# First cross attention: division by the row sums moved from VectorE and TensorE to GpSimd, and the small jobs dealt to other units

## The reference

```python
Q = (x @ WQ_w.T + WQ_b).reshape(b, sq, H, DK).transpose(0, 2, 1, 3)
K = (kv @ WK_w.T + WK_b).reshape(b, sk, H, DK).transpose(0, 2, 1, 3)
V = (kv @ WV_w.T + WV_b).reshape(b, sk, H, DK).transpose(0, 2, 1, 3)
T = jnp.einsum('bhqd,bhkd->bhqk', Q, K) / math.sqrt(DK)
T = T + attn_bias[:, None, :, :]
T = jnp.where(m2[:, None, :, :] == 0, -1000000000.0, T)
A = jax.nn.softmax(T, axis=-1)
out = jnp.einsum('bhqk,bhkd->bhqd', A, V)
out = out.transpose(0, 2, 1, 3).reshape(b, sq, E)
return out @ WO_w.T + WO_b
```

## Time and profile before

| | us |
|---|---|
| median of 3 runs | 2248.33 (2246.73 to 2257.74) |
| the profiled execution | 2246.41 |
| its span | 2244.6 |
| of it the first attention | 0 to 346.6 |
| first scores of batch 1, of batch 2, of batch 3 | 101.48, 179.53, 257.58 |

### The profile page before, as it was taken

One profiled execution on the slowest core, in us unless ns is written; L12 is line 12 of the kernel. 1 busy time (PEld: TensorE's weight loads), 2 busy tenths in 40 slices (PEclk: granted clock), 3 DMA queues, 4 the chain that ended last, 5 costly groups with the idle time before them and its releaser, 6 DMA issues. The chain is left out here.

```text
span 2244.6 us, 45912 instructions
## 1 busy us (share of the span) xinstructions
PE 2172.1 (97%) x18243; PEld 1463.3 (65%) x18276; DVE 1685.6 (75%) x4495; ACT 815.4 (36%) x1943; POOL 178.5 (8%) x427
## 2 busy tenths in 40 slices
PE   7999999999999999998999999999889999999998
PEld 3555554445756756775555555556678989898997
DVE  7888885866566566535887787877698988888895
ACT  4888881311311311302654554545321121111210
POOL 5553201000000000000000000000000000000000
PEclk9999999999999999999999999999999999999999
DMA  5111103000000003001000000001200000000000
GB/s 178 27 39 47 26 10 153 1 1 1 1 1 1 1 0 113 1 1 50 2 1 1 1 1 1 1 1 58 95 1 2 1 11 2 1 11 1 2 11 11
DMA packets 24165, 48.65 MB, mean 22 GB/s; under 512 B 5008, under 2 KB 13456, under 8 KB 22928
## 3 DMA queue, kind: packets, MB, share of 16 engines
q1 hardware_dynamic: 23952, 45.71, 6.1%
HBM read 37.57 MB, written 2.10 MB: 18 GB/s over the span
## 5 line engine op out<-in xcount | busy, mean ns | idle before, releaser
L2286 PE MATMUL banks<-work,big 128*128 128x128 f32 x2048 | 252.7, 277 | 2.0 <-PEq L376 1.3
L2286 PEld LDWEIGHTS banks<-work,big 128*128 128x128 f32 x2048 | 246.2, 193 | 7.6 <-issue 3.2
L614 ACT ACTIVATE work<-banks,work 128x512 f32<-128x512 f32 x256 | 174.8, 687 | 203.9 <-DVE work L731 203.9
L1085 PE MATMUL banks<-big,work 128*128 128x256 f32 x1024 | 241.3, 379 | 3.6 <-issue 3.3
L1009 PE MATMUL banks<-big,work 128*128 128x512 f32 x512 | 228.4, 600 | 1.6 <-DMA big<-in_B_val 1.4
L2379 ACT ACTIVATE work<-banks 128x512 f32<-128x512 f32 x128 | 76.5, 598 | 408.6 <-PE banks L2286 405.3
L1085 PEld LDWEIGHTS banks<-big,work 128*128 128x128 f32 x1024 | 195.0, 190 | 33.9 <-issue 1.9
L1904 ACT ACTIVATE work<-work 128x512 f32<-128x512 f32 x256 | 181.0, 711 | 0.0
L1009 PEld LDWEIGHTS banks<-big,work 128*128 128x128 f32 x512 | 96.0, 191 | 116.0 <-issue 113.3
L731 DVE TENSOR_REDUCE work<-banks 128x2 f32<-128x1024 f32 x128 | 150.4, 1217 | 7.7 <-PE banks L470 7.7
L1307 DVE CUSTOM_DVE_ANT_0 work<-banks,work 128x512 f32<-128x512 f32 (+3 forms) x128 | 57.7, 488 | 121.5 <-PE banks L1025 109.2
(11 more groups left out here) (248 smaller groups left out, 3791.7 us busy)
## 6 DMA issues: line engine op xcount, KB each, us to landing
work<-work SPq DMA_DIRECT2D x152, 32.0 KB, 2.0
big<-in_bias SPq DMA_DIRECT2D x16, 256.0 KB, 4.6
big<-in_B_val SPq DMA_DIRECT2D x8, 512.0 KB, 7.0
big<-in_B_out SPq DMA_DIRECT2D x1, 4096.0 KB, 18.9
big<-in_D_downT SPq DMA_DIRECT2D x4, 1024.0 KB, 5.5
big<-in_D_up SPq DMA_DIRECT2D x1, 4096.0 KB, 15.4
wc<-in_ctxT SPq DMA_DIRECT2D x1, 2048.0 KB, 7.8
wab<-in_L_ffn_w_q SPq DMA_DIRECT2D x1, 2048.0 KB, 10.1
```

Source lines behind the costliest of these rows:

```text
L614: eng.activation(prob[:, n % NS * PAIR + j, :], SB[n % 2][:, j, :], ACT.Exp, bias=low[:, n % NS, j:j + 1], accum_out=rowsum[:, n % NS, j:j ...
L1085: last = eng.matmul(XO[qt // 2][:, qt % 2 * D:(qt % 2 + 1) * D], spread[:, c % NG, qt * P:(qt + 1) * P], w_out[:, c, :], start=False, stop ...
L2286: last = eng.matmul(HP[n % 2][:, q * P:(q + 1) * P], down[:, (n * NJ + q) * KC + kc, :], xnT[par][:, kc, :], start=(kc == 0), stop=(kc == ...
```

## The change

The row sums are no longer collected by ScalarE. They come out of `weigh`, in the rows that belong to the ones. `take_o` writes oT, now in two buffers. `gather_heads` moves, for each group, four times 16 rows of sums and four times 16 rows of heads. `weigh_heads` on GpSimd inverts the sums of a pair of groups (half of `whole`, 128 rows of 512) by three Newton steps and multiplies: one tensor_scalar on integers, three times (tensor_tensor, tensor_scalar, tensor_tensor), one tensor_tensor. There is one buffer of sums, so a pair's gather waits for the weighing of the pair before. `inverses`, L1988 and L1995 are gone, the jobs stand at other i, and the last loop is one turn shorter. A unit without a job gets `keep_busy` as before.

```diff
+def gather_heads(eng, m, heads, whole, sums, g):
+    A = A_
+    for j in range(A.group):
+        r, at = (g % 2 * A.group + j) * A.dk, A.strip * j + A.dk
+        eng.dma_start(sums[r:r + A.dk, :], heads[at:at + A.dk, :]).then_inc(m["A.sums_moved"][g % 2], 16)
+    for j in range(A.group):
+        r, at = (g % 2 * A.group + j) * A.dk, A.strip * j
+        eng.dma_start(whole[r:r + A.dk, g // 2, :], heads[at:at + A.dk, :]).then_inc(m["A.compacted"][g], 16)
+
+def weigh_heads(eng, m, pair, whole, sums, inverse, product, step):
...
+    for moved in m["A.sums_moved"]:
+        eng.wait_ge(moved, 16 * A.group * (pair + 1))
...
+    eng.tensor_scalar(inverse.bitcast(I32), sums.bitcast(I32), -1.0, INVERSE_SEED, ALU.mult, ALU.add).then_inc(step, 1)
+    for k in range(NEWTON):
+        eng.wait_ge(step, n + 3 * k + 1)
+        eng.tensor_tensor(product, inverse, sums, ALU.mult).then_inc(step, 1)
+        eng.wait_ge(step, n + 3 * k + 2)
+        eng.tensor_scalar(product, product, -1.0, 2.0, ALU.mult, ALU.add).then_inc(step, 1)
+        eng.wait_ge(step, n + 3 * k + 3)
+        eng.tensor_tensor(inverse, inverse, product, ALU.mult).then_inc(step, 1)
...
+    eng.tensor_tensor(whole[:, kc, :], whole[:, kc, :], inverse, ALU.mult).then_inc(m["A.weighted"], 1)
...
-    OUT_AT = (5, 6, 10, 12)
+    OUT_AT = (8, 9, 12, 15)
...
-        if i % QT == 3:
-            return ("mult", (n - 7) // QT) if n >= 7 and (n - 7) // QT < B * G else None
-        if i in (0, 1) and b < B:
+        if i in (0, 2) and b < B:
...
-        if more and i in (2, 13):
+        if more and i in (4, 13):
...
-        if more and i in (8, 9):
+        if more and i in (10, 11):
...
-        if more and i in (4, 14):
+        if more and i in (6, 14):
...
-    for n in range(LAST + 4):
+    for n in range(LAST + 3):
...
-                def compact(b, g):
-                    eng.wait_ge(dve_took, TOOK[("mult", G * b + g)])
+                def gather(b, g):
+                    eng.wait_ge(o_taken, G * b + g + 1)
                     if b >= 2:
                         eng.wait_ge(job_made, MADE[("out", b - 2, QT - 1)])
+                    eng.wait_ge(weighted, (G * b + g) // 2)
+                    gather_heads(eng, m, oT[g % 2], whole[b % 2], sums, g)
...
                 for b in range(1, B):
+                    if b >= 2:
+                        eng.wait_ge(row_step, ROWS * (b + 1))
+                        weigh_heads(eng, m, 2 * b - 3, whole[b % 2], sums, mm, bt, m["A.newton_step"])
                     find_root(eng, b)
                     stage_x(b)
...
                         fold_bias(eng, b, t, fold_step, fold_at(b, t) - FOLD, mm, bt)
+                    eng.wait_ge(fold_step, fold_at(b, QT - 1))
+                    weigh_heads(eng, m, 2 * b - 2, whole[(b - 1) % 2], sums, mm, bt, m["A.newton_step"])
                     if b + 1 < B:
+                        eng.wait_ge(weighted, 2 * b - 1)
                         fold_rows(eng, b + 1)
+                weigh_heads(eng, m, 2 * B - 3, whole[B % 2], sums, mm, bt, m["A.newton_step"])
+                weigh_heads(eng, m, 2 * B - 2, whole[(B - 1) % 2], sums, mm, bt, m["A.newton_step"])
...
-                def inverses(g):
...
                 def outputs(b, t, bank):
                     bank_free(eng, ("out", b, t))
                     if t == 0:
-                        for g in range(G):
-                            eng.wait_ge(compacted[g], 16 * GH * (b + 1))
+                        eng.wait_ge(weighted, 2 * b + 2)
...
-                    eng.activation(one, one, ACT.Exp, bias=low[:, n % 2, j:j + 1], scale=-1.0,
-                                   accum_out=rowsum[:, n // QT % 2, at:at + 1]).then_inc(p_ready, 1)
+                    eng.activation(one, one, ACT.Exp, bias=low[:, n % 2, j:j + 1], scale=-1.0).then_inc(p_ready, 1)
```

More of the change, by code:

```diff
@@ L982, in late_output @@
                     if t == 0:
[L983 to L984 removed]
+                        eng.wait_ge(m["A.weighted"], 2 * B)
                         eng.wait_ge(val_scaled.sem, val_scaled.at(0, VU))
```

123 lines of the change are left out of this document (50 added, 73 removed).

## The result

The changed kernel takes 2255.98 us (median of 12 runs, 2251.8 to 2261.69); beside it, the kernel before took 2250.94. The ratio is 1.0026, with a 95% interval of 1.0015 to 1.0037; in a second series of runs it was 1.0021 (1.0009 to 1.0034). Two of the twelve runs of before, of 2495.76 and 6567.85 us, do not enter the ratio. So it is slower by a quarter of a per cent, clear of zero but within the 0.5% that counts as no change here. I had predicted 2250.0 with a range of 2243 to 2261. The measured time lies in the range, but above the band of 2245 to 2255 that I had given 0.62, and the difference between the two profiled executions is 7.9 us where the sum had 2.6.

What follows compares the result with a forecast made beforehand. The prediction took TensorE's loop, with its wait for ScalarE's copy, as the bound in the first cross attention. Its terms, -1.4 - 3.0 + 2.5 + 4.5 = +2.6 on 2246.4, gave 2249.0; it predicted 2250.0 us, range 2243 to 2261.

Steps and rivals of the forecast that it cites:

- the sum: All terms together: +2.6 us on the profiled execution's 2246.4 us.
- The units: First cross attention: units still last 4.64 us (short job) and 5.27 us (long job), so relieving VectorE and ScalarE gains 0.
- The start, -1.4: First units of the attention: unit 1 loses its long job, 2.0 us gained by unit 4, 0.6 given back in unit 6.
- The end, -3.0: End of the first cross attention: the last loop turn goes, with its spread of inverses and two unused matmuls; 3.0 us less.
- The next block, +2.5: Start of the next block: SyncE issues eight moves, not four, ahead of the value experts' loads; TensorE waits 2.5 us more.
- The weighing's waits, +4.5: First outputs of batches 2 and 3: TensorE waits for GpSimd's 13.3 us weighing; 4.5 us more, slow SyncE issues included.
- The second: Rival: GpSimd's weighing becomes the loop's bound, with waits at first outputs of batches 1 to 3; 2261 us, chance 0.12.
- The first: Rival: GpSimd is never late with its weighing; sum -1.9, 2244.5 us or 2246 on the median's scale, chance 0.21.
- the third: Rival: VectorE bounds the units, so its multiplications and reciprocals come back whole, 14.9 us; 2231.5 us, chance 0.05.

Runs made afterwards that it cites:

- before_relieved: The kernel before without row-sum readouts on ScalarE and with VectorE's division multiplying 16 columns only; 2249.87 us, ratio 1.0000 to before.
- start_busy: The changed kernel with two unused matmuls also in the job-less units from 1 on (units 1 and 3); 2254.41 us, ratio 1.0012 to before.
- both: The changed kernel with block B's value-expert loads issued early and the last group's heads of the batch before collected early; 2247.38 us, ratio 0.9991 to before.
- Loads_first: The changed kernel with SyncE issuing block B's value-expert loads ahead of the first cross attention's last gather; 2247.96 us, ratio 0.9990 to before.
- before_loads_first: The kernel before with block B's value-expert loads issued ahead of the first cross attention's last moves; 2246.84 us, ratio 0.9986 to before.
- Gather_early: The changed kernel with the gather of the previous batch's last group moved ahead of the key moves and bias loads; 2249.62 us, ratio 1.0002 to before.
- newton4: The changed kernel with four Newton steps instead of three in GpSimd's weighing; 2274.54 us, ratio 1.0106 to before.

## Why the prediction was right or wrong

**The units, right.** 4.64 and 5.27 us as forecast, and before_relieved shows the reason: relieving VectorE and ScalarE changes nothing.

**The start, -1.4: wrong.** Unit 7 began at 59.49 instead of 58.44. From the first scores to it are 39.72 us (39.27 before), each with 3.41 us of half clock; over all profiles, with half of the half clock taken off, this part takes 37.2 to 38.1 us in either kernel. In the kernel before, unit 1 with its long job starts at 28.43 and goes on so:

```profile
30.15 1.98 PE L1729 MATMUL banks<-big,wab 128*128 128x512 f32 x4
32.06 0.71 PE L1808 MATMUL banks<-ident,work 64*128 64x64 f32 x16
32.71 1.14 PE L1794 MATMUL banks<-work 16*128 16x512 f32 x8
```

That is 4.28 us, against 3.94 without the job. Taking it out left an idle time of 1.21 us, which ScalarE's copy ends, and a gain of 0.34 us. The step that failed is the one that counted all of TensorE's 1.98 us as time of the path: most of the job stood in a wait for ScalarE, as a short job does wholly (start_busy: 3.93 us with 1.12 us of unused matmuls). Unit 2 gains too (4.43 us at full clock, in the profile of both, against 5.10 before), but later units give it back, unit 6 among them (5.28 us in place of 4.64).

**The end, -3.0: right.** 17.93 became 15.02 us: -2.91.

**The next block, +2.5: the mechanism right, the size too small.** The wait grew by 3.42 us, not 2.5: the four moves more took 2.5, SyncE began 0.5 later, and the load landed 4.69 us after its issue began, where 4.2 had been enough (346.64 + 2.41 to 353.23); TensorE came to it 0.2 later itself. The clock was taken at nothing, and it fell longer: 10.24 us at 1.2 GHz where before it was 6.83. The Trainium skill (TensorE: Matmul & The Clock Gate, Part 1) says that the clock follows how busy the array has recently been, by which a longer wait makes the longer slow stretch likelier. The traces agree: seven profiled kernels with the loads behind eight moves have 10.24 us at this place six times and 6.83 once, the two with four moves have 6.83, and the five with the loads in front have 0, 3.41, 3.41, 6.83 and 6.83. The upper end that I had given, +4.4, was nearer than the value that I took.

**The weighing's waits, +4.5: right in place, too large.** Nothing in batch 1, 1.96 in batch 2, 0.33 in batch 3, 2.3 in all (2.7 in the mean of six profiles). The weighing takes 12.2, not 13.3 us: its integer operation runs in 0.62 us, not in L1515's 1.50, which turns integers into f32. The weighing in batch 2 begins 31.2 us into the batch instead of 28.7, so the 2.5 us that I had added were needed, but slow issues were the smaller part of them. The queue took 17.9 us from its first gather to the sums (188.06 to 205.91), where my terms give 17.1. The rest came behind the issues: the weighing starts 5.9 us after 205.91, not 3.8, as the sums' moves land after 3.5 to 3.8 us in place of 1.9 to 2.0. They stand behind four bias loads; the DMA engines' share is 0.92 from 205.9 to 209.0. This points to the bias loads as the cause. So the shorter weighing and the later start nearly cancelled, and that the sum for batch 2 came near is luck in part. Batch 3's chain had a slip: its own terms give 9.6 for the "9 or so", and with it 1.7 us of lateness, not 1.1. The rule on shared interfaces (the Trainium skill, GPSIMD Engine Reference, section 1) speaks of VectorE instructions with two SBUF inputs or in a 2-port perf mode; VectorE's long instructions here read a PSUM bank, so no run tests it. No slowing is seen: the 18 multiplications of L1425 in six weighings average 1276 ns, like L1532's 1279.

**The sum.** At full clock my terms come out as 0 - 2.9 + 1.7 (half of the added wait) + 2.3 = +1.1, and the runs gave +1.0. They agree more closely than the reading's error of 0.4 us allows to tell. What the sum lacked is the clock: 4.5 us in the mean, which took the time above the band that I had thought likeliest; the wide range held it. Loads_first gives the clock back (.9940, the same as before_loads_first's .9941), so without the late loads that loss is gone. Gather_early gives half of it back too (.9929), and both edits together (.9933) no more than loads_first, so the two shares don't add, and how the clock falls beyond the next block's start isn't settled. The 2.24 us waits at the batches' ends are followed by half clock in 15 of 18 places in the unfilled kernels with the loads behind eight moves and in 8 of 15 in the other unfilled ones, which points to the late loads but is too few to show it.

**The rivals.** The second, that the weighing becomes the bound, needed 14.5 us and got 12.2; newton4, at 15.7, shows the mechanism real and the sum of its waits priced nearly right (15.7 us against 16.7, whose own terms add up to 16.6), with the clock's share left out. The first failed by the two waits, the third by before_relieved.

## What to carry to other kernels

When work is moved to a DMA queue, ask first what stands behind it in that queue: four more moves ahead of the next block's loads added 3.4 us of wait, more than the moved arithmetic did in the same profile (2.3). A wait's price has two parts, its length and the clock behind it: loads_first took out 4.8 us of wait and gained 7.8. Put the loads that the next stage waits for at the head of the queue, and small moves that something waits for ahead of large loads. Where a producer's lateness delays its own next input, its slack is worth more than its length says: beyond the edge 3.5 us cost 13. And size a filler by its instructions in the trace, not by its calls.

## What the runs showed of the hardware that I had not expected

- TensorE's clock: half-clock stretches appear in the traces in lengths of 3.41, 6.83 and 10.24 us, and the same program differs from run to run (mean clock .989 to .994 for the changed kernel, 2250.7 to 2261.7 us over its 24 runs).
- An unchanged idle time of 2.24 us is sometimes followed by half clock and sometimes not.
- GpSimd's operation on 128x512 integers with integer output takes 618 ns in the mean of six; the one with f32 output takes 1.50 us.
- Moves of 16x512 landed 2.8 to 3.8 us after their issue behind four bias loads of 256 KB (batches 1 and 2), and 1.9 to 2.0 us without such loads (batch 3).
- The unused matmuls at the attention's end (3.3 us) bought no clock: .9917 without, .9918 with them.
